# Expert pass of a graph network: W_out folded into the strong experts' second matrices, in the pass's first step

## The reference, cut to what matters

```python
for l in range(3):
    agg = segment_sum(h[src], dst, num_segments=N) / deg
    logits = concatenate([h, agg], axis=-1) @ router_W[l] + router_b[l]
    gate_dense = the softmax of the two largest logits, at their places, zero elsewhere
    weak = relu(einsum('nh,ehf->nef', agg, weak_W[l]) + weak_b[l])          # 4 experts, 256 -> 256
    sh = relu(einsum('nh,ehf->nef', agg, strong_W1[l]) + strong_b1[l])      # 4 experts, 256 -> 512
    strong = einsum('nef,efh->neh', sh, strong_W2[l]) + strong_b2[l]        # 512 -> 256
    moe = einsum('ne,neh->nh', gate_dense, concatenate([weak, strong], axis=1))
    h = h + sigmoid(h @ conf_W[l] + conf_b[l]) * moe
return h @ W_out + b_out                                                    # 256 -> 128
x = x + that                      # then layernorm, relu, and the next network's h @ W1 + b1
```

## Time and profile before

| | us |
|---|---|
| median of 3 runs | 7056.86 (7054.11 to 7063.53) |
| span of the profiled execution, first to last instruction | 8283.1 |
| PE busy in the span | 6772.3 (82%) |
| DVE busy | 3911.7 (47%) |
| POOL busy | 3351.8 (40%) |
| ACT busy | 2104.7 (25%) |
| third expert pass, one step | 29.9 |

### The profile page before, as it was taken

The page is one execution under the profiler, slowest core; times in us unless marked ns, Lnnn a source line. Parts: engine busy times, 40 slices in busy tenths (PEclk is TensorE's granted clock), DMA queues, the critical chain, the costliest instruction groups (busy, mean ns, idle before and its releaser), DMA issues. The chain is left out here.

```text
span 8283.1 us, 149959 instructions
## 1 busy us (share of the span) xinstructions
PE 6772.3 (82%) x51098; PEld 4970.7 (60%) x51098; DVE 3911.7 (47%) x11484; ACT 2104.7 (25%) x6166; POOL 3351.8 (40%) x3404
## 2 busy tenths in 40 slices
PE   4999768888886888888688888867767766989899
PEld 2555457676775677677567776755555554545455
DVE  7777534444443444444344554446666662112111
ACT  3555312222221222222133333322222220000000
POOL 0000055555554555555455555536666661000000
PEclk6999879999997999999799999975555557999999
DMA  5444355554444544445444444434444445656565
GB/s 152 139 119 126 115 160 145 143 143 140 140 129 148 143 142 140 138 143 147 133 135 138 141 138 136 139 89 124 128 124 124 126 124 187 196 170 198 175 202 161
DMA packets 714971, 1188.63 MB, mean 144 GB/s; under 512 B 258882, under 2 KB 512998, under 8 KB 712163
## 3 DMA queue, kind: packets, MB, share of 16 engines
q0 software_dynamic: 200640, 601.97, 26.1%
q1 hardware_dynamic: 466786, 447.42, 18.0%
q10 hardware_dynamic: 46784, 129.65, 4.4%
HBM read 993.57 MB, written 185.20 MB: 142 GB/s over the span
## 5 line engine op out<-in xcount | busy, mean ns | idle before, releaser
L557 POOL DMA_INDIRECT ring<-parts,src_idx x2496 | 2452.0, 982 | 1950.7 <-PE sums L707 687.1
L1209 PEld LDWEIGHTS hid<-agg,big 128*128 128x128 f32 x9408 | 1155.6, 196 | 140.2 <-issue 105.9
L1209 PE MATMUL hid<-agg,big 128*128 128x128 f32 x9408 | 1190.6, 280 | 58.8 <-issue 43.5
L2360 PE MATMUL agg_ps<-sheet,big 128*128 128x448 f16 x6174 | 1196.4, 354 | 33.6 <-DMA sheet<-adj 33.6
L1170 PE MATMUL y<-big,strong 128*128 128x256 f32 x4704 | 1126.2, 387 | 40.6 <-issue 21.3
L557 POOL DMA_INDIRECT ring<-rows_yh,src_idx x832 | 838.0, 1007 | 565.4 <-issue 220.3
L677 DVE TENSOR_TENSOR acc<-acc,sums 128x128 f32 x624 | 180.3, 289 | 1678.6 <-DMA acc<-in_edge_type 1171.4
L2360 PEld LDWEIGHTS agg_ps<-sheet,big 128*128 128x128 bf16 x6174 | 605.9, 99 | 582.5 <-DMA sheet<-adj 35.8
L1170 PEld LDWEIGHTS y<-big,strong 128*128 128x128 f32 x4704 | 862.7, 191 | 150.9 <-issue 51.4
L1093 ACT ACTIVATE strong<-hid,s_b 128x128 f32<-128x128 f32 x2352 | 665.3, 368 | 892.6 <-PE hid L1209 615.2
L707 PE MATMUL sums<-onehot,ring 128*128 128x64 bf16 x14976 | 614.5, 196 | 284.1 <-issue 211.6
(11 more groups left out here) (377 smaller groups left out, 8497.9 us busy)
## 6 DMA issues: line engine op xcount, KB each, us to landing
sheet<-adj SPq DMA_DIRECT2D x294, 784.0 KB, 4.2
ring<-parts,src_idx POOLq DMA_INDIRECT x2496
adj<-big ACTq DMA_DIRECT2D x7, 5488.0 KB
adj<-acc ACTq DMA_DIRECT2D x7, 5488.0 KB
hp<-parts SPq DMA_DIRECT2D x147, 192.0 KB
relb<-rel_rows ACTq DMA_DIRECT2D x106, 256.0 KB
parts<-cut SPq DMA_DIRECT2D x99, 192.0 KB, 1.8
h<-rows SPq DMA_DIRECT2D x147, 128.0 KB
```

What stands on the lines that cost most here:

```text
L557: nc.gpsimd.indirect_dma_start(ring[:, k, 0:YH] if edge_net else ring[:, k, :], None, table, bass.IndirectOffsetOnAxis(ap=src_idx[:, i * R ...
L1209: ins = nc.tensor.matmul(p["hid"][:, bank_at, j * P:(j + 1) * P], w["s1"][:, k, e, j * P:(j + 1) * P], s["agg"][:, k, :], start=(k == 0), ...
L2360: last = nc.tensor.matmul(ps[:, g % 2, 0:HALF_COLS], now[:, b, c, :], sheet[:, k, s * HALF_COLS:(s + 1) * HALF_COLS], start=(b == 0 and c ...
```

## The change

In the first step of the third pass a new generator (fold) multiplies each strong expert's s2 (512 x 256), and the four strong biases, with W_out: PE turns eight pieces of 128 x 128, ACT copies them, PE makes four products of 128 columns (two pieces each), DVE copies those into s2_out and down_b_out. Five such rounds are spread over places 5 to 15 of the step. All blocks then use s2_out: down0 to down3 have 128 columns. Their mixes and those of the biases go into part (128 columns, begun from b_out), and only h and the weak experts into row, which is therefore finished in the middle of a block: row_t moves to place 10, h_out to place 14, and with_row adds its result. The late part ends with mix6 and mix7 and goes straight to new_x; its further places move from 8 and 15 to 4 and 9, and h2_t and h2_w from 12 and 14 to 6 and 8. s2 is loaded ahead of the other weights in this pass. The first two passes keep their order.

The diff, cut to its core:

```diff
                          "pe_result", "act_result", "dve_result", "pe_late", "act_late", "dve_late",
                          "small_loaded", "large_loaded", "down_loaded"]
+                if not edge_net:
+                    names += ["fold_pe", "fold_act", "fold_dve", "fold_own"]
...
-                                step(0, [])
+                                step(0, [work.fold(eng)] if work.LATE else [])
...
+        class Layer1Out(Layer1):
...
+            FOLDS = NW + 1
+            PE = "h_t weak0 logits weak1 up0 up1 down0 up2 row_t down1 up3 h_out"
+            ACT = "cleared h_t_sb relu_w0 exps relu_w1 relu0 relu1 relu2 row_t_sb relu3"
+            DVE = Layer1.ROUTE + "mix0 mix1 mix2 mix3 down_b0 down_b1 down_b2 down_b3 mix4 mix5 with_row"
+            PE_LATE = "down2 down3 h2_t h2_w"
+            ACT_LATE = "norm_root h_row h2_t_sb"
+            DVE_LATE = "mix6 mix7 new_x " + Work.NORM_DVE + " next_y y_b1" + Work.CUT + " next_h"
...
+            def fold_pe(self, pe):
+                s, p, w = *self.b, self.w
+                def turned(n):
+                    bank = self.fold_banks(n)
+                    for a in range(2):
+                        for k in range(4):
+                            src = (w["s2"][:, k, n, a * P:(a + 1) * P] if n < NW else
+                                   w["down_b"][:, k, a * P:(a + 1) * P])
+                            ins = nc.tensor.transpose(bank[:, a, k * P:(k + 1) * P], src, ident[:, :])
+                    ins.then_inc(self.sem["fold_pe"], 1)
+                def product(n):
+                    pe.wait_ge(self.sem["fold_act"], n + 1)
+                    if n:
+                        pe.wait_ge(self.sem["fold_dve"], n)
+                    for k in range(4):
+                        for a in range(2):
+                            ins = nc.tensor.matmul(p["hid"][:, 2, k * D:(k + 1) * D], w["turned"][:, n % 2, a, k * P:(k + 1) * P],
+                                                   self.last["w_out"][:, a, :], start=(a == 0), stop=(a == 1))
+                    ins.then_inc(self.sem["fold_pe"], 1)
+                yield 5
+                pe.wait_ge(self.sem["down_loaded"], w["down"])
+                turned(0)
+                for n in range(1, self.FOLDS):
+                    yield 5 + 2 * n
+                    if n == NW:
+                        pe.wait_ge(self.sem["small_loaded"], w["small"])
+                    turned(n)
+                    product(n - 1)
+                yield 15
+                product(NW)
+            def fold_act(self, act):
+                w = self.w
+                for n in range(self.FOLDS):
+                    yield 5 + 2 * n
+                    act.wait_ge(self.sem["fold_pe"], 2 * n if n else 1)
+                    bank = self.fold_banks(n)
+                    for a in range(2):
+                        ins = nc.scalar.copy(w["turned"][:, n % 2, a, :], bank[:, a, :])
+                    ins.then_inc(self.sem["fold_act"], 1)
+            def fold_dve(self, dve):
+                w = self.w
+                for n in range(self.FOLDS):
+                    yield 7 + 2 * n
+                    dve.wait_ge(self.sem["fold_pe"], 2 * n + 3 if n < NW else 2 * NW + 2)
+                    made = self.b[1]["hid"][:, 2, :].rearrange("p (k d) -> p k d", d=D)
+                    nc.vector.tensor_copy(w["down_b_out"] if n == NW else w["s2_out"][:, :, n, :], made
+                                          ).then_inc(self.sem["fold_dve"], 1)
+            def folded(self, eng):
+                eng.wait_ge(self.sem["fold_dve"], self.FOLDS)
...
+            def on_act(self, act, m, i, b, added):
...
+                yield 12
+                m.need(self.pe, "row_t")
+                m.done("row_t_sb", nc.scalar.copy(s["rt"][:, :, :], p["misc"][:, 0:H].rearrange("p (a j) -> p a j", j=P)))
+                yield 14
+                self.relu_strong(m, 3)
+            def on_dve(self, dve, m, i, b, added):
+                s, p = self.b
+                row, part = s["row"][:, :], s["part"][:, :]
+                yield from self.route_dve(dve, m, b, added)
+                yield 7
+                m.need_before(self.pe, "row_t")
+                m.need(self.act, "relu_w0")
+                self.mix(m, "mix0", row, s["weak"][:, 0, :], 0, s["h"][:, :])
+                self.mix(m, "mix1", row, s["weak"][:, 1, :], 1, row)
+                yield 8
+                m.need(self.act, "relu_w1")
+                self.mix(m, "mix2", row, s["weak"][:, 2, :], 2, row)
+                self.mix(m, "mix3", row, s["weak"][:, 3, :], 3, row)
+                yield 9
+                if self.in_pass:
+                    self.folded(dve)
+                for e in range(NW):
+                    self.mix(m, f"down_b{e}", part, self.w["down_b_out"][:, e, :], NW + e, part if e else self.last["b_out"])
+                yield 10
+                m.need(self.pe, "down0")
+                self.mix(m, "mix4", part, p["y"][:, 0, 0:D], NW, part)
+                yield 13
+                m.need(self.pe, "down1")
+                self.mix(m, "mix5", part, p["y"][:, 1, 0:D], NW + 1, part)
+                yield 15
+                m.need(self.pe, "h_out")
+                m.done("with_row", nc.vector.tensor_tensor(part, part, p["misc"][:, 0:D], ALU.add), wait=True)
+            def down(self, m, e):
+                s, p, w = *self.b, self.w
+                y = p["y"][:, e % 2, 0:D]
+                for k in range(4):
+                    ins = nc.tensor.matmul(y, s["strong"][:, e % 2, k, :], w["s2_out"][:, k, e, :], start=(k == 0), stop=(k == 3))
+                m.done(f"down{e}", ins)
...
+            def on_pe(self, pe, m, i, b, added):
+                s, p = self.b
+                w = self.w
+                yield 2
+                if self.in_pass:
+                    self.folded(pe)
+                yield from self.route_pe(pe, m, "with_row")
+                yield 5
+                self.up(m, 0)
                 yield 6
-                m.need(self.pe2, "h_out")
-                m.done("x_part", nc.vector.tensor_tensor(s["u"][:, :], p["misc"][:, 0:D], self.last["b_out"], ALU.add), wait=True)
...
+                yield 10
+                m.need(self.dve, "mix3")
+                m.need_before(self.dve2, "y_b1")
+                for a in range(2):
+                    ins = nc.tensor.transpose(p["misc"][:, a * P:(a + 1) * P], s["row"][:, a * P:(a + 1) * P], ident[:, :])
+                m.done("row_t", ins)
...
+                yield 14
+                m.need(self.act, "row_t_sb")
+                for k in range(2):
+                    ins = nc.tensor.matmul(p["misc"][:, 0:D], s["rt"][:, k, :], self.last["w_out"][:, k, :],
+                                           start=(k == 0), stop=(k == 1))
+                m.done("h_out", ins)
+            def late_pe(self, pe, m, i, b, routed):
+                s, p = self.b
+                yield from super().late_pe(pe, m, i, b, routed)
+                yield 6
+                if routed:
+                    pe.wait_ge(self.dve.sem, self.dve.at("logits_sb", i + 1))
+                m.need(self.act2, "h_row")
+                m.done("h2_t", nc.tensor.transpose(p["misc"][:, 0:P], s["hn"][:, :], ident[:, :]))
+                yield 8
+                m.need(self.act2, "h2_t_sb")
+                m.done("h2_w", nc.tensor.matmul(p["misc"][:, 0:D], s["hnt"][:, :], self.last["w1"], start=True, stop=True))
...
+            def late_dve(self, dve, m, i, b):
+                s, p = self.b
+                part, x, st = s["part"][:, :], s["x"][:, :], s["st"]
+                yield 1
+                m.need(self.pe2, "down2")
+                self.mix(m, "mix6", part, p["y"][:, 0, 0:D], NW + 2, part)
+                yield 2
+                m.need(self.pe2, "down3")
+                self.mix(m, "mix7", part, p["y"][:, 1, 0:D], NW + 3, part)
                 dve.wait_ge(self.sem["late_in"], i * 16 + 16)
-                m.done("new_x", nc.vector.tensor_tensor(s["x"][:, :], s["x"][:, :], s["u"][:, :], ALU.add), wait=True)
-                x, st = s["x"][:, :], s["st"]
+                m.done("new_x", nc.vector.tensor_tensor(x, x, part, ALU.add), wait=True)
...
-                yield 8
+                yield 4
                 m.need(self.act2, "norm_root")
...
-                yield 15
+                yield 9
                 m.need(self.pe2, "h2_w")
...
+                "turned": big[:, 1, 0:2048].rearrange("p (n a j) -> p n a j", n=2, a=2),
+                "s2_out": big[:, 1, 2048:4096].rearrange("p (k e d) -> p k e d", k=4, e=NW),
+                "down_b_out": big[:, 1, 4096:4608].rearrange("p (e d) -> p e d", e=NW),
...
+                def load_down():
+                    for k in range(4):
+                        rows = slice(k * P, (k + 1) * P)
+                        go(w["s2"][:, k, :, :], t["L1_gnn_strong_W2"][l, :, rows, :].rearrange("e p f -> p e f"), down)
+                if l == 2:
```

(54 more changed lines are left out.)

188 lines of the change are left out of this document (116 added, 72 removed).

## The result

The changed kernel takes 6976.55 us (median of four runs, 6969.36 to 6977.91), the kernel before beside it 7058.64: ratio 0.9881, 95% interval 0.9868 to 0.9893, 82 us less. The forecast was 6965.

A forecast was written before the change was run, and what follows sets the result against it. PE was taken to set the third pass, gathers being a floor. Profile terms -173 - 65 + 120 + 6 - 8 = -120 scaled to -102; floors gave -91, start and tail -2: -92, 6965 us, range 6875 to 7045.

The forecast's parts named there:

- the floors: Third pass with prompt signals: PE's 23.7 us a step before, 21.8 after from PE 21.0 and gathers 21.1; -91.
- The step of 27 to 28 us and the clock of 0.9: Signs expected in the third pass of the trace after the change: step 27 to 28 us, clock at 0.9.
- The scaled sum of -102: Terms summed in the profile's own time, -120 of 8283 us, scaled with 0.852 to the runs.
- Down products: Third pass, PE: 32 records a step go from 256 to 128 columns, saving 3.6 us a step, -173.
- The end of the step: DVE between last add and agg: next_y to next_h leave, with_row enters; -1.6 us where PE waits, -65, bounds 0 and -75.
- The row's wait: PE mid-step at row's transpose, for mix3 and y_b1: 2.5 us, +120, bounds +43 and +210; as slower rival, chance 0.07.
- The norm chain: DVE behind agg, mix6 to statistics: costs 0; bound +2 us a step (+96) if x loads late; new_x waiting disproves prediction.
- The fold: First step of third pass: 13.4 us of PE work, double at half clock, covered by gathers; +6, bounds 0 and +25.
- The full PE saving: Rival, third pass: no wait at row_t, agg earlier by all of 1.6 us; -204 scaled, 6853 us; chance 0.18.
- The gathers did not pace the pass before: Rival: gathers already pace the third pass, or nearly; small gain -15 to -45 (chance 0.14) or nothing (0.07).
- the clock was 1.00: Rival, third pass: waits drop PE's clock to 0.50; if for half the pass, +290, 7347 us; chance 0.04.
- Late signals: Sums reaching DVE late, 3.9 us before one add against 0.44 elsewhere; a skill's rule would ascribe this to profiling.

The follow-up runs named there:

- new order, wide products: Changed kernel with the third pass's down products 256 columns wide again, the other 128 columns of each unused: 7052.55 us, ratio 0.9986.
- Narrow work without the order: Kernel before with two of the four pieces of each down product in the third pass, other half left out: 7022.41 us, ratio 0.9943.
- run with the late cut: Changed kernel with the cut and next_h (1.4 us of DVE) moved back behind the step's last add, ahead of agg: 7169.28 us, ratio 1.0147.
- run with fewer gathers: Every fourth gather of the third pass replaced by a POOL clear: changed kernel 6987.0 us (0.9894), kernel before 7072.09 us (1.0014).

## Why the prediction was right, and where it wasn't

**The total.** The forecast came from the floors: 23.7 us a step before, set by PE, and 21.8 after, with PE and gathers near each other. Measured: 23.26 with PE busy throughout, and 21.54, the gathers' 21.44. The two floors after were each off: PE's work and waits were taken as 21.0, and its work alone is 20.2 (882 of 940 us at 21.54 a step); the gathers were taken as 21.1, from 1.25 us a gather, and one takes 1.274. That the 0.7 us allowed on top came out so near is partly luck. The step of 27 to 28 us and the clock of 0.9 that were named for the trace after belonged to the disturbed execution. In the two profiles the pass's steps give (23.24 - 21.53) x 47 = -80, the start +1 (+6 taken), and from the last block's first product to the edge pass's first gather 67.9 in place of 80.8 us, -13 (-8 taken). Together -92 of the 94.6 between the spans; the medians differ by 82. The scaled sum of -102 lies near as well, by luck alone: its +120 for the row's wait measured 12, and its -173 and -65 arrive in part.

**Down products.** Right: the burst has 2.03 us for 3.70, and by busy time a record goes from 309.4/1297 to 183.9/1400 us, which over 32 records is 3.4 us. Only half of that arrives, 1.72 us a step, since the gathers take over.

**The end of the step.** This step failed. I read agg's lateness from the add that followed its sums by 3.9 us, and gave the move -65. In the undisturbed profile the add follows by 0.13 us and the burst hides the chain: the move by itself saves 10 us at most (new order, wide products). The floors have no term for it, so the forecast was not hurt. The move is needed for another reason, which I hadn't seen: the products that become shorter are the cover of that chain. Narrow work without the order is worth 40, the order without it 10, both 82; and 1.3 us put back ahead of agg cost 57.

**The row's wait.** Its place and its releaser (y_b1, L1545) were right, the size wrong: 2.5 us taken, also from the late signals; 0.26 measured, under the lower bound of 0.9, and worth nothing when it is moved away.

**The norm chain.** Nothing, as taken, but by a small margin: new_x waited for x's load 14.9 us in 44 steps, up to 1.8. The prediction had named that wait as a sign of being wrong; PE never waited for the chain behind it. The run with the late cut shows a wait of over 5 us there, and if the 136 us that the order doesn't account for are its price, the bound of +2 us a step was too low.

**The fold.** Hidden, as named, with the cover used up.

**The rivals.** The full PE saving (6853) is stopped by the gathers, as the argument against it said: with 1.8 us a step less for PE nothing is won. The gathers did not pace the pass before: POOL had waits of up to 3.0 us for the sums there, and fewer gathers gave no gain. The row's wait stayed small, and the clock was 1.00. In the run with the late cut the clock can be seen to fall: the stretch behind a wait of 2.50 us has 0.53, nearly all of it at the lower level, and the 16 up products in it take 3.58 us in place of 1.95. It is not so behind each such wait: in 20 of 36 steps these products took 2.7 to 3.6 us, in the others 1.95, as behind the 2.60 us below. A step with the fall, the clock of it, and a step without:

```profile
3801.28 0.34 PE L1481 MATMUL misc<-ident,hn 128*128 128x128 f32 x1 [2.50 <-ACT hn L1514]
3801.42 3.58 PE L1201 MATMUL hid<-agg,big 128*128 128x128 f32 x16
...
3801.40:3805.00 3.60, 3.60 (x23) 3.54 (x23) 1.61 (x8) 2.95 (x8) 0.00 (x0) 0.53 0.19 55
...
4110.30 0.30 PE L1481 MATMUL misc<-ident,hn 128*128 128x128 f32 x1 [2.60 <-ACT hn L1514]
4110.44 1.95 PE L1201 MATMUL hid<-agg,big 128*128 128x128 f32 x16
```

The Trainium skill's "TensorE: Matmul & The Clock Gate", section "HAM oscillation — how this bites in real kernels", says that waits between bursts of matmuls put the clock back; the trace agrees in the steps where it fell.

**Late signals and the recording.** I ascribed the lateness to the profiling, beside a sentence of the Trainium skill's "NOTIFIC — the notification-queue block", section "Overflow: three behaviours, one of which stalls the engine", by which the block that writes the records holds back its producers inside rather than lose one. The kernel before, recorded again, has a span of 7062.2 us beside a median of 7062.7, so no run here shows that recording delays signals. Why that one execution was disturbed stays open. The floors were the right base, for the reason that they don't rest on its waits.

**Open.** That POOL's gathers pace the changed pass is read from their unbroken row, which fills the step, and from PE's edits: less work for PE gave nothing, and where DVE's chain grew the row had gaps and the time went up. A run with a quicker row of gathers and nothing else changed was not had. In the run with fewer gathers PE's waits came to 1.7 us a step beside the same work, with DVE held up as well, so what a quicker POOL would give stays open.

## What to carry to other kernels

When work is taken from the engine that sets the pace, ask what that work was hiding: half of this gain exists only because the chain behind the shortened burst was shortened in the same change. Work out the next engine's floor before counting the saving, since here 3.4 us of work became 1.7 of time. If a profiled execution is far above the runs, profile it again before its waits are put into a sum.

## What the runs showed of the hardware

Beside a clear of 128x768 bf16 on POOL (0.76 us) DVE's 128x128 cast to bf16 took up to 1.51 us in place of 0.23. The 0.30 us between two gathers stay with no wait and no other instruction written between them. In the run with fewer gathers a clear starts right at the end of a gather, with a wait and an empty instruction written between them, and the next gather 0.17 us behind the clear:

```profile
3699.94 0.94 POOL L562 DMA_INDIRECT ring<-parts,src_idx  x1 [0.30 <-issue]
3700.88 0.76 POOL L560 MEMSET ring<- 128x768 bf16 x1
3701.80 1.07 POOL L562 DMA_INDIRECT ring<-parts,src_idx  x1 [0.17 <-issue]
...
3700.30 1.42 DVE L902 CAST cut<-left 128x128 bf16<-128x128 f32 x1
```

In the changed kernel DVE stands 0.92 us between with_row and agg in the step shown; what for was not tried.
